# Grouped attention of layer 2: value mixes of one key tile at a time, or of two

## The reference

```python
def _L2_xattn_ref(q, k, v):
    B, S, E = (2, 512, 512)
    QH, KVH = (32, 8)
    D = E // QH
    G = QH // KVH
    b, s, _ = q.shape
    qh = q.reshape(b, s, KVH, G, D).transpose(0, 2, 3, 1, 4)
    kh = k.reshape(b, s, KVH, D).transpose(0, 2, 1, 3)
    vh = v.reshape(b, s, KVH, D).transpose(0, 2, 1, 3)
    scale = 1.0 / jnp.sqrt(jnp.float32(D))
    scores = jnp.einsum('bkgsd,bktd->bkgst', qh, kh) * scale
    attn = jax.nn.softmax(scores, axis=-1) / DROPOUT
    out = jnp.einsum('bkgst,bktd->bkgsd', attn, vh)
    return out.transpose(0, 3, 1, 2, 4).reshape(b, s, E)
...
x = x + jnp.tanh(g_xattn[2]) * _L2_xattn_ref(_layernorm(x, axis=-1), ctx_512, ctx_512)
```

## Time and profile before

| | |
|---|---|
| median of 3 runs | 3749.89 us (3747.46 to 3751.34) |
| the profiled execution | 3746.39 us |
| its span, first to last instruction | 3744.6 us |
| mean granted clock of TensorE | 0.976 |
| TensorE busy | 3525.3 us, 94% |
| VectorE busy | 2176.8 us, 58% |
| ScalarE busy | 1403.8 us, 37% |
| GpSimd busy | 627.6 us, 17% |

### The profile page before, as it was taken

How to read it: one execution, slowest core, us unless ns; L and a number is a source line. 1 busy time by engine, 2 the same in 40 slices (tenths; PEclk the granted TensorE clock), 3 DMA queues, 4 the chain that set the end, 5 groups by cost and what they waited for, 6 DMA issues and landing times.

```text
span 3744.6 us, 38074 instructions
## 1 busy us (share of the span) xinstructions
PE 3525.3 (94%) x12973; PEld 1932.4 (52%) x12974; DVE 2176.8 (58%) x3832; ACT 1403.8 (37%) x2908; POOL 627.6 (17%) x589
## 2 busy tenths in 40 slices
PE   5999999996889999599979999999999999999999
PEld 2444444442444444256634444444444445888888
DVE  7657676135677777411137776666675665655554
ACT  7525252111456666322224343444444443111111
POOL 5100000000132322211110100000000002544543
PEclk7999999998889999799989999999999999999999
DMA  7321311310422332455551201010101002121120
GB/s 238 135 75 68 130 68 68 116 45 23 109 53 57 80 75 57 173 157 165 159 186 55 72 26 38 26 38 26 39 26 38 26 26 101 57 68 57 68 79 23
DMA packets 81559, 292.46 MB, mean 78 GB/s; under 512 B 17897, under 2 KB 18793, under 8 KB 66545
## 3 DMA queue, kind: packets, MB, share of 16 engines
q1 hardware_dynamic: 74016, 267.74, 21.9%
q0 software_dynamic: 7376, 22.57, 2.0%
HBM read 246.74 MB, written 38.81 MB: 76 GB/s over the span
## 4 chain that ended last, share of the span: by engine, by line
PE 88%; DVE 6%; POOL 2%; ACT 1%; DMA 1%; issue 1%; SPq 0%; DVEq 0%; ACTq 0%; POOLq 0%
PE BM L2402 6%; PE BM L2472 6%; PE BM L460 6%; PE BR L460 6%; PE BM L2843 4%; PE BS L2843 3%; PE BR L2843 3%; PE BT L1616 3%; PE BT L2464 3%; PE BT L476 3%; PE BR L2481 3%; PE BS L476 3%; PE BM L2423 3%; PE BR L2055 3%; DVE NEG L1771 3%; PE BM L2044 3%
## 5 line engine op out<-in xcount | busy, mean ns | idle before, releaser
L2540 ACT COPY AR<-BM 128x512 f32<-128x512 f32 x320 | 187.2, 585 | 275.1 <-PE BM L2472 100.1
L228 POOL TENSOR_TENSOR RSTD<-VAR,HALF 128x4 f32<-128x4 f32 x31 | 33.5, 1082 | 1414.0 <-DVE VAR L2666 895.4
L2472 PE MATMUL BM<-AR 128*128 128x512 f32 x512 | 246.5, 593 | 0.0
L2402 PE MATMUL BM<-XT,AR 128*128 128x512 f32 x512 | 237.4, 607 | 0.0
L460 PE MATMUL BM<-XT,AR 128*128 128x512 f32 x512 | 230.2, 594 | 0.9 <-ACT AR L625 0.9
L460 PE MATMUL BR<-XT,AR 128*128 128x512 f32 x512 | 230.2, 593 | 0.0
L1709 ACT ACTIVATE PT<-BS 128x512 f32<-128x512 f32 x340 | 192.9, 600 | 90.6 <-PE BS L1606 85.2
L2546 ACT ACTIVATE AR<-BS,AR 128x512 f32<-128x512 f32 x128 | 86.8, 683 | 333.4 <-DVE AR L2636 333.4
L632 ACT ACTIVATE AR<-AR 128x512 f32<-128x512 f32 x256 | 182.6, 714 | 76.3 <-DVE AR L760 72.2
L2464 PEld LDWEIGHTS BT<-ID,AR 128*128 128x128 f32 x1024 | 127.3, 140 | 137.6 <-issue 133.1
L1771 DVE TENSOR_REDUCE NEG<-BM 128x2 f32<-128x1024 f32 x129 | 157.6, 1222 | 65.6 <-PE BM L1590 63.4
(11 more groups left out here) (460 smaller groups left out, 7241.2 us busy)
## 6 DMA issues: line engine op xcount, KB each, us to landing
AR<-l_wq_dram SPq DMA_DIRECT2D x32, 1152.0 KB, 5.1
AR<-l_w_dram SPq DMA_DIRECT2D x36, 1024.0 KB, 4.8
AR<-l_w_dram SPq DMA_DIRECT2D x64, 512.0 KB, 3.2
AR<-l_w_dram SPq DMA_DIRECT2D x40, 768.0 KB, 4.8
AR<-w2h SPq DMA_DIRECT2D x16, 1024.0 KB, 4.8
QS<-qx SPq DMA_DIRECT2D x32, 512.0 KB, 9.2
AR<-l_w_dram SPq DMA_DIRECT2D x8, 1408.0 KB, 8.3
made<-AR SPq DMA_DIRECT2D x40, 256.0 KB, 4.9
```

Of the source, the lines that this page charges most:

```text
L2402: last = nc.tensor.matmul(bank, WS[:, p % 2, at:at + P], XT[:, b % 2, kt, :], start=kt == 0, stop=kt == KT - 1)
L2472: last = nc.tensor.matmul(BM[:, L3[job] % 2, :], KVN[:, p // 8 * ST + lt, :], PROBT3[:, lt, :], start=lt == 0, stop=lt == ST - 1)
L2540: nc.scalar.copy(to, BM[:, L3[job] % 2, :]).then_inc(m_free, 1)
```

## The change

Behind h = 1 of every key tile but the first two, TensorE now does the mix of one key tile, the one two key tiles back. Before, it did two behind h = 1 of every second key tile, those of three and of two key tiles back. The last two mixes, behind the loops, stay together as they were. No other engine's order is touched; lines below the edit move up by one.

```diff
                         shifted(n, tt, h)
                         if n + 2 < NG:
                             scores(n + 2, 2 * tt + h // 2, h % 2)
-                        if h == 1 and tt % 2 == 1 and ST * n + tt > 1:
-                            for t in range(2):
-                                mix(*divmod(ST * n + tt - 3 + t, ST))
+                        if h == 1 and ST * n + tt > 1:
+                            mix(*divmod(ST * n + tt - 2, ST))
                         if tt == 2 and h == 1 and n:
                             turn_out(n - 1)
```

## The result

The changed kernel takes 3724.86 us (median of 4 runs, 3721.58 to 3727.33) where the kernel before takes 3750.11 (4 runs): 25.2 us less, a ratio of 0.9933, 95% interval 0.9916 to 0.9950. That is faster by more than the 0.2% which can be told from no change, close to the 3723 that stood on record and well inside its range.

A forecast was written before the change was run, and what follows sets the result against it. The prediction took TensorE, stalled by unevenly fed VectorE, as the bound: 45.9 us of stalls less 21.4 of switches, about -25 us, gave 3721 from the profile and 3725 from the median; predicted 3723, range 3710 to 3744.

The forecast's parts named there:

- uneven feeding: In the attention stage, a double visit of mixes leaves VectorE idle 1.75 us, then TensorE stalls because only two units fit.
- Rival 1: TensorE is the bound and 63 added switches of 0.34 us simply add: 3771 us; chance 0.13.
- Rival 2: No change: the stalls move to ScalarE, which frees the exponential banks; with half of them staying 3748 us; chance 0.09.
- The price of a lone visit: On TensorE, 0.86 us for one key tile's mix plus 0.34 into the 32-column form and back: 1.20 us.
- The plain group: A group with nothing beside its attention: 13.94 us, 1.48 of it stall, becomes 13.14 us, 0.80 less.
- the walk through one visit: Following each unit's bank behind a lone mix: free by about 1.7 us, wanted at about 2.6, so no stall.
- I let them cancel: Groups with more VectorE work gain more, those waiting for routing less; 0.80 us for all 31 intervals, 24.8 us.
- 45.9 of stalls less 21.4: Over the stage: 31 x 1.48 us of stalls go, 63 x 0.34 us of switches come; about -25 us.
- the forecast's own range: From 3711 us, with groups losing up to 1.2 us, to 3736, with a lone visit costing half as much again in switching.
- a price twice as high: Far bound of a lone visit, twice the switching price, 1.54 us in all: the kernel would still gain 4 us.
- TensorE needs 3.06 us a key tile and VectorE 2.28: Work per key tile with lone visits: TensorE 8 x 0.233 + 1.20 us, VectorE 2 x 1.14 us.

The follow-up runs named there:

- near: Against the kernel before: the two mixes of every second key tile stand singly behind h = 0 and h = 1, not spread evenly; 3769.2 us.
- quick kernels: Each maximum reads 128 of the 512 keys: on the kernel before with double visits 3705.1 us, on the changed kernel with lone visits 3706.3 us.
- lone_h0: Against the changed kernel: lone visits stand behind h = 0 of each key tile, in the middle of a score unit; 3763.0 us.
- quad: Against the kernel before: all four mixes of a group stand together, behind h = 1 of the next group's first key tile; 3772.7 us.

## Why the prediction was right

**What bounds the stage.** That uneven feeding, not TensorE's 94%, was the point is shown: near keeps the lone visits without it and loses 20 us, and between the quick kernels the difference is gone. Rival 1 (the switches simply add) is what near measured, 3769 where 3771 was written; it did not come in the changed kernel because the stalls went. Rival 2 did not come: ScalarE is fed more evenly as well (idle for 0.97 us in place of 1.92).

**The price of a lone visit.** 1.66 us from matmul to matmul was worked out from a double visit, 1.65 was measured, and near's median gives 0.32 us a switch against 0.34.

**The plain group.** 13.14 us was written, 12.98 measured: 0.96 less than before in place of 0.80. Its stalls were sized rightly (1.48 us written, 1.5 counted) and went completely, as the walk through one visit said. The 0.16 us lie in TensorE's own work: a step taken as 0.233 is nearer 0.231 (32 of them), and the output transposes now stand directly behind a mix, so that one way back serves both: from 1105.71 to 1107.76 are 2.05 us, 0.40 more than a lone visit without transposes, where 0.45 was counted.

**All groups.** "I let them cancel" was right in the sum (24.3 us in the stage, 24.8 written), and that was luck, for its parts are far apart. Groups with a norm became up to 1.7 us shorter; groups with routing 0.1 to 0.4 us shorter, or 0.5 longer; the first and the last interval stayed as they were. In one of those with routing that became longer, 14.66 us where before had 14.16, VectorE's routing steps now fall where TensorE needs a bank:

```profile
1252.50 0.51 PE L1590 MATMUL BM<-KS,QS 128*128 128x512 f32 x1 [0.67 <-DVE NEG L1770]
```

**The two terms.** "45.9 of stalls less 21.4" held as a sum and not in its make-up. The price held: near paid 20.4 us for the 63 visits. The stalls that went are about 41 us by the count of long steps, and 24.3 + 20.4 = 44.7 us if everything beside the price is put down to them; the steps that got shorter and the shared way back, named above, lie between the two. But 45.9 stood for all stalls, 1.48 us in each of 31 intervals. There were about 65 us, more than was written, and 24 of them stayed; that these two errors cancel is luck as well.

Nor were the stalls all VectorE's, as the argument had it. By the quick kernels, VectorE cost the stage 466.5 - 423.1 = 43.4 us before, and still costs 442.2 - 428.2 = 14.0 after: 29.4 went. The other 12 or so of the 41 us are of the kind that double visits keep with a fast VectorE. Lone visits take them away, too, and so the 63 switches cost only 428.2 - 423.1 = 5.1 us there, by one profile of each, in place of 20.4. The prediction has no term for this: it names ScalarE only as a rival that would keep the gain away.

Three of its sums are off by up to 2 us, without consequence: 45.9 - 21.4 is 24.5 and not 24.8; the lower end of the forecast's own range is counted from 3748 and the upper from 3750; and a price twice as high would leave a gain of 3 us, not 4.

**What the argument left out.** "TensorE needs 3.06 us a key tile and VectorE 2.28" stands beside the walk through one visit as if it, too, told that the stalls go. It does not: lone_h0 has the same two numbers and a plain group of 15.2 us. Only the walk through one visit, with the time at which each bank is free and wanted, decides, and of the three places tried (h = 0, 1 and 3) it holds for h = 1 alone.

## What to carry to other kernels

Where an engine feeds another through two buffers and also does long work of another kind, cut that work into pieces that the consumer can bridge, and put each piece where the consumer has a full unit in hand and its next buffer is not wanted soon; the place was worth 38 us here (lone_h0 against the changed kernel), more than the cutting. Price the cut first, from the matmul ahead of the piece to the second one behind it. A busy share near 95% can hide such stalls, as here; distances between the starts of an engine's instructions, and a consumer that idles and is waited for in turn, show them.

## What was not expected of the hardware

The way into the 32-column form and back costs the same whether one key tile is mixed, two or four: 0.33 and 0.34 us in the timelines of the changed kernel and of the one before, 0.34 in quad (4.24 us from 1101.63 to 1105.87, less two steps of 0.23 and 4 x 0.86), and 0.32 by 63 visits more in near. Transposes with 8 columns of weights between full matmuls show no such price ahead of them: they start one usual step of 0.23 us behind the matmul before (1103.80 to 1104.03 in the earlier trace rows).
